# Moving more of a gather to TensorE, and half of its one-hots to ScalarE, in the second layer of a graph network

## The reference, cut to what matters

```
h = relu(layernorm(x));  x = x + segment_sum(h[src] * edge_weight, dst)
h = relu(layernorm(x));  s, v = h[:, :8], h[:, 8:].reshape(n, 8, 3)
w = (relu(edge_attr_32 @ W1 + b1) @ W2 + b2).reshape(e, 4, 8, 8)
m0, m1 = products of s[src], v[src], edge_attr_4 and w          # 8 and 8 x 3 per edge
x = x + concat(segment_sum(m0, dst) + s @ si_w0, segment_sum(m1, dst) + v @ si_w1)
```

## Time and profile before

| | us |
|---|---|
| median of 3 runs (lowest, highest) | 9337.08 (9321.34, 9354.07) |
| the profiled execution's own time | 9330.14 |
| its span, first to last instruction | 9328.3 |
| TensorE busy | 7326.0 (79%) |
| TensorE's weight loads busy | 4946.4 (53%) |
| VectorE busy | 5420.8 (58%) |
| ScalarE busy | 3091.8 (33%) |
| GpSimd busy | 4880.8 (52%) |
| mean granted clock of TensorE | 0.856 |

### The profile page before, as it was taken

How to read it: one execution, slowest core, us unless ns; L and a number is a source line. 1 busy time by engine, 2 the same in 40 slices (tenths; PEclk the granted TensorE clock), 3 DMA queues, 4 the chain that set the end, 5 groups by cost and what they waited for, 6 DMA issues and landing times.

```text
span 9328.3 us, 170251 instructions
## 1 busy us (share of the span) xinstructions
PE 7326.0 (79%) x46802; PEld 4946.4 (53%) x46802; DVE 5420.8 (58%) x12253; ACT 3091.8 (33%) x13298; POOL 4880.8 (52%) x5215
## 2 busy tenths in 40 slices
PE   6888888888888886777777777777777777777777
PEld 5777777676777775444444444444444444444444
DVE  6666666666666665555555555555555555555555
ACT  2222222222222222433433343333333433333334
POOL 4666656666666665444444444444444444444444
PEclk9999999999999997788888888888888888888887
DMA  3111111111111111111111111111111111111111
GB/s 81 25 26 25 26 25 26 25 26 25 26 26 26 25 25 26 28 22 23 22 22 23 23 23 22 21 22 22 22 22 23 22 23 22 22 23 22 22 23 23
DMA packets 376870, 235.14 MB, mean 25 GB/s; under 512 B 114825, under 2 KB 373209, under 8 KB 376333
## 3 DMA queue, kind: packets, MB, share of 16 engines
q0 software_dynamic: 163424, 84.00, 6.9%
q1 hardware_dynamic: 212428, 147.61, 6.2%
q10 hardware_dynamic: 990, 3.21, 0.1%
HBM read 229.19 MB, written 5.23 MB: 25 GB/s over the span
## 4 chain that ended last, share of the span: by engine, by line
PE 30%; another core or an unknown queue 26%; issue 18%; DVE 18%; DVEq 5%; ACT 2%; DMA 0%; ACTq 0%; POOL 0%; POOLq 0%; SPq 0%
PE w_ps L696 22%; DVE prod L1174 4%; DVEq L993 3%; DVE t L1179 2%; PE w_ps L706 2%; PE hp_ps L824 2%; PE w_ps L777 2%; DVE z L1211 1%; DVE reduced_sb L1142 1%; DVE acc L1000 1%; DVE reduced_sb L1139 1%; DVE prod L1183 1%; DVE vsh L1158 1%; DVE pick L1010 1%
## 5 line engine op out<-in xcount | busy, mean ns | idle before, releaser
L446 POOL DMA_INDIRECT z<-h_table,idx x5107 | 4836.7, 947 | 4359.1 <-DVE prod L1183 2015.2
L696 PE MATMUL w_ps<-parts,pick 128*128 128x448 f32 x11662 | 2766.0, 390 | 355.2 <-issue 284.1
L696 PEld LDWEIGHTS w_ps<-parts,pick 128*128 128x128 f32 x11662 | 2284.4, 201 | 635.7 <-issue 422.0
L548 ACT ACTIVATE z<-z,squares 128x32 f32<-128x32 f32 x3125 | 798.4, 311 | 2758.1 <-issue 2511.8
L824 PE MATMUL hp_ps<-parts,pick 128*128 128x448 f32 x4340 | 1190.6, 413 | 50.7 <-issue 48.6
L1164 DVE TENSOR_TENSOR p<-w_ps,scalars 128x320 f32<-128x320 f32 x625 | 302.9, 485 | 1498.9 <-remote 1486.7
L824 PEld LDWEIGHTS hp_ps<-parts,pick 128*128 128x128 f32 x4340 | 857.8, 211 | 283.5 <-issue 224.1
L599 ACT ACTIVATE hid<-w_ps,b_sb 128x320 f32<-128x320 f32 x625 | 329.6, 527 | 1946.0 <-remote 1702.7
L777 PE MATMUL w_ps<-w_sb,hid 64*128 64x256 f32 x5000 | 929.9, 497 | 5.2 <-issue 4.3
L1010 DVE TENSOR_TENSOR pick<-sc_ps,feat 128x896 fp32r<-128x896 f32 x833 | 889.7, 1089 | 52.6 <-issue 44.6
L793 PE MATMUL sc_ps<-prod,onehot 128*32 128x344 f32 x5000 | 672.1, 475 | 300.1 <-issue 168.1
(11 more groups left out here) (96 smaller groups left out, 6429.1 us busy)
## 6 DMA issues: line engine op xcount, KB each, us to landing
z<-h_table,idx POOLq DMA_INDIRECT x5107
feat<-key_table SPq DMA_DIRECT2D x311, 192.0 KB
ft_sh_sb<-in_ft_sh SPq DMA_DIRECT2D x625, 90.0 KB
feat<-key_table SPq DMA_DIRECT2D x210, 64.0 KB
h_table<-big SPq DMA_DIRECT2D x10, 280.0 KB
rel_sb<-in_dst_t SPq DMA_DIRECT2D x1, 1562.5 KB
idx_all<-in_src_t SPq DMA_DIRECT2D x1, 1532.5 KB
squares<-in_ew_t SPq DMA_DIRECT2D x1, 1532.5 KB, 12.5
```

The lines of the kernel that those rows point to most:

```text
L446: pool.indirect_dma_start(z[:, r, u, :], None, rows, bass.IndirectOffsetOnAxis(ap=idx[:, r, u:u + 1], axis=0)).then_inc(z_in[r], 16)
L548: last = nc.scalar.activation(z[:, r, u, :], z[:, r, u, :], ACT.Copy, scale=ew_all[:, bass.ds(n * G + u, 1)])
L696: mm = pe.matmul(fold_ps[:, pick_banks[k], 0:NC * D], pick[:, k, blk, :], parts[:, t, :, blk, :], start=(blk == 0 and t == 0), stop=(blk = ...
```

## The change

The second layer takes the pattern of period three. Of three supertiles, those with r % 3 = 1 and 2 have their fifth tile gathered by TensorE; the one with r % 3 = 0 has all five tiles by GpSimd.

- TensorE: in iteration r % 3 = 0 the whole gather (14 matmuls) for the supertile two ahead; in r % 3 = 1 the first 6 matmuls for the one three ahead; in r % 3 = 2 the other 8.
- The one-hots of the r % 3 = 1 tiles are still made by VectorE (L1192's instruction), in iterations r % 3 = 0. Those of the r % 3 = 2 tiles are made by ScalarE, at the end of its iterations r % 3 = 1: per block |row - key| by an Abs (7 of them, 128 x 128, into `far`, a free part of `squares`), then one Relu of 1 - far over 896 columns into `pick`.
- VectorE selects for both: for the r % 3 = 1 tile at select(), for the r % 3 = 2 tile behind the reductions, the sum right behind it.
- Keys: four for a body of six, in two transfers of two, after VectorE's and ScalarE's picks of the body before.

```diff
     def on_pe(r):
-        return r % 2 == 0
+        return r % PERIOD > 0
...
-                    count = PEG if s is None else min(PEG, (S - (s - r + R1) + 1) // 2)
-                    if count > 0:
-                        sp.wait_ge(pick1_ready, nth(b, r) + 1)
+                    most = R1 if s is None else min(R1, S - (s - r + R1))
+                    if most > 1:
+                        sp.wait_ge(pick1_ready, b * (PAIRS1 // 2))
                         sp.nop(nofuse=True)
-                        load_keys1(first, count)
+                        sp.wait_ge(pick1_by_act, b * (PAIRS1 // 2))
+                        sp.nop(nofuse=True)
+                        load_keys1(first, most)
...
+            def make_pick1(b, r, s):
+                base, e = 0 if s is None else s - r, PERIOD - 1
...
+                act.wait_ge(keys1_in, b * (16 * R1 // PERIOD) + 16 * loads)
+                if s is None or s >= R1:
+                    act.wait_ge(picked1, nth(b, r, e) + 1)
+                for blk in range(GB):
+                    last = nc.scalar.activation(far[:, blk], key1[:, slot1(r, e)], ACT.Abs, scale=-1.0, bias=rows_sb[:, blk:blk + 1])
+                last.then_inc(pick1_far, 1)
+                act.wait_ge(pick1_far, b * (R1 // PERIOD) + r // PERIOD + 1)
+                nc.scalar.activation(pick[:, slot1(r, e)], far, ACT.Relu, scale=-1.0, bias=one_sb[:]).then_inc(pick1_by_act, 1)
...
                 nc.scalar.activation(onehot[:, v], near[:], ACT.Relu, scale=-1.0, bias=one_sb[:]).then_inc(hot1_ready, 1)
+                if r % PERIOD == 1:
+                    make_pick1(b, r - 1, None if s is None else s - 1)
...
-                    ahead = 2 if on_pe(r) else 3
+                ahead, blocks = ((2, range(GB)), (3, range(GB // 2)), (2, range(GB // 2, GB)))[r % PERIOD]
...
-                    if not on_pe(r):
-                        pe.wait_ge(pick1_ready, i + 1)
-                        if s is None or s > 3:
+                    if blocks[0] == 0:
+                        if r % PERIOD == 0:
+                            pe.wait_ge(pick1_by_act, half_nth(b, r, ahead) + 1)
+                        else:
+                            pe.wait_ge(pick1_ready, half_nth(b, r, ahead) + 1)
+                        if s is None or s > 4:
                             pe.wait_ge(group1_step, i * 2)
...
-                selects = not on_pe(r) and (s is None or R1 <= s + 3 < S)
+                selects = on_pe(r) and (s is None or R1 < s + 3 < S)
                 def select():
-                    if selects:
+                    if selects and r % PERIOD == 1:
                         select_group1(b, r)
...
                     if selects:
+                        if r % PERIOD == 2:
+                            select_group1(b, r)
                         sum_groups1(b, r)
```

More of the change, by code:

```diff
@@ L65, in gnn_two_layers @@
     assert J % JG == 0 and S // R0 >= 2 and GU >= 2
+    PAIRS1 = R1 // PERIOD * (PERIOD - 1)
+    assert R1 % PERIOD == 0 and PAIRS1 <= SLOTS
     assert AW % 2 == 0 and R0 % PERIOD == 0 and NPE == S + S // PERIOD
@@ L401, in load1, with load_keys1 @@
                 sp.dma_start(ft_sh_sb[:, r, :], ft_sh[n]).then_inc(ft_in[r], 16)
-                def load_keys1(first, count):
-                    sp.dma_start(key1[:, 0:count, :], key_dram[bass.ds(first, count, 2)].rearrange("s a e -> a s e")
-                                 .to_broadcast([P, count, P])).then_inc(keys1_in, 16)
+                def load_keys1(first, most):
+                    for p in range(R1 // PERIOD):
+                        count = min(PERIOD - 1, most - p * PERIOD - 1)
+                        if count > 0:
+                            t = slot1(p * PERIOD + 1)
+                            sp.dma_start(key1[:, t:t + count, :],
+                                         key_dram[bass.ds(first + p * PERIOD + 1, count)].rearrange("s a e -> a s e")
+                                         .to_broadcast([P, count, P])).then_inc(keys1_in, 16)
                 if s == R1 - 1:
@@ L608, in scale_rows @@
                 last.then_inc(coef_ready, 1)
+            def make_pick1(b, r, s):
+                base, e = 0 if s is None else s - r, PERIOD - 1
+                if s is not None and s + e + R1 >= S:
+                    return
+                loads = R1 // PERIOD if s is None else sum(base + R1 + p * PERIOD + 1 < S for p in range(R1 // PERIOD))
+                act.wait_ge(keys1_in, b * (16 * R1 // PERIOD) + 16 * loads)
[6 more added lines that the diff above has]
+                nc.scalar.activation(pick[:, slot1(r, e)], far, ACT.Relu, scale=-1.0, bias=one_sb[:]).then_inc(pick1_by_act, 1)
             def edge_rows(b, r, s):
@@ L1184, in products, with make_picks1 @@
                                         sh1.unsqueeze(2).to_broadcast([P, G, MUL, 3]), ALU.mult).then_inc(msg1_ready, 1)
-            def make_pick1(b, r, s):
-                t = r // 2
-                dve.wait_ge(keys1_in, (b + 1) * 16)
-                if s is None or s >= R1:
-                    dve.wait_ge(picked1, nth(b, r) + 1)
-                nc.vector.tensor_tensor(pick[:, t], rows_ps.unsqueeze(2).to_broadcast([P, GB, P]),
-                                        key1[:, t].unsqueeze(1).to_broadcast([P, GB, P]), ALU.is_equal
-                                        ).then_inc(pick1_ready, 1)
+            def make_picks1(b, r, s):
+                base = 0 if s is None else s - r
+                loads = R1 // PERIOD if s is None else sum(base + R1 + p * PERIOD + 1 < S for p in range(R1 // PERIOD))
+                for e in (1,):
+                    if s is None or s + e + R1 < S:
+                        dve.wait_ge(keys1_in, b * (16 * R1 // PERIOD) + 16 * loads)
+                        if s is None or s >= R1:
+                            dve.wait_ge(picked1, nth(b, r, e) + 1)
+                        nc.vector.tensor_tensor(pick[:, slot1(r, e)], rows_ps.unsqueeze(2).to_broadcast([P, GB, P]),
+                                                key1[:, slot1(r, e)].unsqueeze(1).to_broadcast([P, GB, P]), ALU.is_equal
+                                                ).then_inc(pick1_ready, 1)
             def select_group1(b, r):
```

36 lines of the change are left out of this document (22 added, 14 removed).

## The result

| | before | after |
|---|---|---|
| median (lowest to highest of 4 runs each), us | 9345.58 (9321.34 to 9365.66) | 9266.8 (9263.76 to 9269.96) |
| ratio, 95% interval | | 0.9917 [0.9891, 0.9942] |
| profiled execution, us | 9330.14 | 9269.96 |

A second comparison on another chip gave 9124.82 for 9194.01 us, ratio 0.9929 [0.9908, 0.9949]. So the change brings 60 to 80 us: inside the likeliest case's own range of 8990 to 9290, but under half of the 200 forecast.

The account below looks back on a forecast made before the run. TensorE's signals, held during runs of GpSimd gathers, were taken as the bound. Terms -0.63 - 0.4 + 0.16 + 0.2 = -0.67 us per three supertiles, times 208 -140, plus -50: 9330 - 190 = 9140, stated as 9145; range 8860 to 9600.

Parts of the forecast that it names:

- TensorE's signals are held while gathers follow one another: Both layers: TensorE's signals come through only 1.2 to 1.9 us after a run of GpSimd gathers ends.
- A run of 4 costs nothing visible: Second layer: a lone group of 4 GpSimd gathers causes no visible wait, judged from the run 5023.86 to 5028.55.
- GpSimd, -0.63 as half a gather: GpSimd, second layer: 13.0 gathers for 13.5 per three supertiles, -0.63 us, a mean between 1.25 and nothing.
- VectorE +0.16, outside its waits: VectorE: half a one-hot less (-0.54) and half a selection more (+0.70) per three supertiles, +0.16 us on its path.
- L1204 no longer waited for, -0.4: VectorE after a wake: its wait for TensorE's gather, 1.65 us a cycle, goes; a quarter counted as gained, -0.4.
- Second selection behind the reductions, 0 of 0 to 1.4: VectorE: the late second selection delays TensorE's next half gather by 0 to 1.4 us per three supertiles; taken as 0.
- ScalarE +0.2: ScalarE's added one-hot work, 3.9 us per three supertiles, costs between 0 and +2.4 us; taken as +0.2.
- TensorE's 7 matmuls at 0: TensorE: 7 more gather matmuls per three supertiles cost between 0 and +2.9 us; taken as 0.
- Runs coming apart, -50: GpSimd's long runs: TensorE's longer iteration sometimes separates the two groups of a run, worth -50 us over the layer.
- TensorE's own stalls: Rival, chance 0.15: stalls come from TensorE's instruction stream, so its added matmuls count outside them, +440 us, 9770.
- The whole gather in the recovery: Rival, chance 0.17: TensorE's 14 matmuls fall right after a wake at half clock; 9640 if all cycles lock, 9490 with half.
- Evens out: Rival, chance 0.10: whole kernel within 0.3%, 9310 to 9365; half a gather won, as much lost in waits.

Follow-up runs that it names:

- early one-hot: Changed kernel with VectorE's one-hot of r%3=0 made before its wait for the window sums: 8840.82 us, ratio 0.9619 to the kernel before, on a holding chip.
- few gathers: Changed kernel with only 2 GpSimd gathers a supertile in the second layer, the others left out: 7184.75 us (kernel before: 9176.12).
- paced kernel: Changed kernel, GpSimd waiting after each second-layer group's second gather for an earlier ScalarE ReLU: ratio 0.9347 on a holding chip, 0.988 where signals aren't held.

## Why the prediction was off, by its own steps

- *TensorE's signals are held while gathers follow one another.* Right on the holding chips. In seven waits of eight the wakes of after came in the pauses, mostly 1.1 us behind a run of 4 and 2.0 behind one of 9, with the added gathers 2.2 behind one of 11; runs of 2 (2.2 us long) cost nothing.
- *A run of 4 costs nothing visible.* Wrong, and this is the step that failed. I judged it from one example in which nothing long was waited for. There VectorE's supertile has no one-hot and waits for TensorE's gather instead; in the other kind of cycle, also in the earlier trace rows, with a lone run of 5, the lone stretch has the wait of 4.77 us at L1192 and lasts 9.69 us from start to start for 7.84. After the change every lone run meets the one-hot, which waits 3.41 us for its held signal. With one gather less in the lone run the kernel was 2.7 us a cycle faster, with the one-hot in front of the wait 1.37.
- *GpSimd, -0.63 as half a gather, as a mean over where it goes.* The run got shorter by this much, and it was the lone run, where by my own reading it was worth nothing. I had forecast that the long run stays 5 + 4 = 9 gathers, as it was; then the gather can't go there. The two sentences contradicted each other and I took the mean of them.
- *VectorE +0.16, outside its waits.* Too small: behind a held signal its order counts, +0.12 in the pause and +0.28 after the wake. The early one-hot alone was worth 1.37 us a cycle, a price that the sum had no term for.
- *L1204 no longer waited for, -0.4.* The wait fell, by more than the quarter that I had priced, from 62.1 us in 1000 to this:

```profile
L1249 DVE TENSOR_TENSOR squares<-hp_ps,group_hot 128x448 f32<-128x448 f32 x76 | 47.5, 625 | 3.5 <-PE hp_ps L866 1.0
```

  but nothing came of it. In the pause the one-hot's held signal took its place, and the way from the wake to the release did not get shorter (5.10 and 5.45, now 5.56): the selection and its sum moved into it.
- *Second selection behind the reductions, 0 of 0 to 1.4.* That it costs nothing is not shown, as its 1.39 us now lie between each wake and the release; but it is the better place: early it costs 1.28 us a cycle more.
- *ScalarE +0.2.* Nothing here contradicts it on a holding chip: giving its one-hots to VectorE loses 0.67 where the whole of VectorE's 1.09 could have been lost, so 0.4 at most was its price if all of it lay on the path. Its rows confirm 0.386 and 1.042 us for the estimated 0.40 and 1.1; but the seven Abs overlap and take 2.14 us together (81.2 us for 38 of them), not 2.8:

```profile
L641 ACT ACTIVATE squares<-feat,rows_sb 128x128 f32<-128x128 f32 x266 | 81.2, 386 | 0.0
...
L644 ACT ACTIVATE pick<-squares,one_sb 128x896 fp32r<-128x896 f32 x38 | 39.6, 1042 | 1.2
```

- *TensorE's 7 matmuls at 0.* Nearly right: by the matmuls taken out, 7 x 0.03 = 0.2 us.
- *Runs coming apart, -50.* This came close, at -58 by the count above; the runs with 4 of the 14 matmuls (199 runs of 8 or 9 for 144) speak for the reason that I gave, TensorE's longer iteration, though its size was a guess. It is the sum inside the cycle that failed: -0.67 us forecast, -0.18 measured.

Of the rivals, TensorE's own stalls fell with the few gathers. The whole gather in the recovery did not occur in the locked cycle. After the wake at 5503.51 TensorE has the 6 matmuls, at half clock as in the earlier trace rows, and the 14 fall under the run of 9 (one record is apart from these 13):

```profile
5508.93 2.49 PE L866 MATMUL hp_ps<-parts,pick 128*128 128x448 f32 x6
...
5520.70 2.91 PE L866 MATMUL hp_ps<-parts,pick 128*128 128x448 f32 x13
```

"Evens out" named a half gather won and as much lost in waits, and the locked cycle shows 0.64 won and 0.46 lost again; its time was 0.5% too high. "Runs come apart" is the direction of most that was gained, at a tenth of its price.

Open: why four chips of five hold the signals and one does not, whether GpSimd's issuing or the gathers' packets hold them, and whether plain transfers issued by GpSimd would in a longer run. The changed kernel itself was not run on the chip that does not hold.

## What to carry to other kernels

When a stall repeats, list every kind of cycle with the length of each part before pricing a change; one example of "costs nothing" is not a price. If signals are held, move work from behind a wait for one to in front of it, and break long runs of GpSimd gathers with a wait that the other engines satisfy: here the first took 3.1% off the changed kernel and the second 5.9%, where moving half a gather had taken 0.8. If your own forecast says where a saved instruction goes, price it there and don't average over the other places.

## What the hardware showed that I had not expected

The same program took 6560 us on one chip and 9176 to 9344 us on four others, with a GpSimd gather 0.94 to 0.95 us long (median) on all of them. The first layer suffers too: in the stretch from 1000 to 3000 us TensorE is busy 1897.83 us at a clock of 0.98 on the one (here in the paced kernel, whose first layer is unchanged), against the earlier trace rows on the other:

```profile
1000.00:3000.00 2000.00, 1897.83 (x12183) 1626.63 (x12181) 1530.56 (x3171) 583.77 (x2685) 1501.91 (x1616) 0.98 0.16 33
```

While signals are held TensorE slows as well: the 8 matmuls of the window sums, 0.79 us in the earlier trace rows, come one by one during the run of 9, here in the changed kernel, where the granted clock is 1.00 from 5520 to 5526 us and 0.78 from there to 5530, so the clock alone is not the reason:

```profile
5525.97 0.45 PE L831 MATMUL sc_ps<-prod,onehot 128*32 128x344 f32 x1 [1.06 <-issue]
5526.68 0.47 PE L831 MATMUL sc_ps<-prod,onehot 128*32 128x344 f32 x1 [0.26 <-issue]
5528.09 0.64 PE L831 MATMUL sc_ps<-prod,onehot 128*32 128x344 f32 x1 [0.94 <-issue]
```

And a gather's price is not its 1.25 us: 0.89 in the long run, 1.35 when one is added to each group, 2.7 where its going breaks a lock.
